# Two tiles of tokens per expert step, with the weights as the stationary operand

## The chip, the cores and the metric

The kernel runs on one core of one Trainium2 chip. The metric is the device time of one execution in microseconds (us); lower is better. Engines are named as in the profile: PE is the matrix engine (PEld its weight loads), DVE the vector engine, ACT the scalar engine, POOL the general engine, SP the queue engine that issues most DMAs.

## The reference

A batch of 32 images (3 x 96 x 96) is cut into 36 patches each, turned into 192-wide tokens, and joined with 128 text tokens: 32 x 164 = 5248 tokens. Then comes one attention block with a decaying state, and a mixture of experts, on which the change works:

```python
xn = _rms_norm(x, norm_w)
xf = xn.reshape(-1, D)                       # 5248 tokens x 192
logits = xf @ router_w.T                     # 8 experts
probs = jax.nn.softmax(logits, axis=-1)
_, top_idx = jax.lax.top_k(probs, TOP_K)     # 2 experts for each token
sel = jax.nn.one_hot(top_idx, N_EXPERTS, dtype=probs.dtype).sum(axis=1)
comb_w = probs * sel
g = jnp.einsum('td,efd->tef', xf, gate_w)    # 192 -> 384 in each expert
u = jnp.einsum('td,efd->tef', xf, up_w)
h = jax.nn.silu(g) * u
h = h * comb_w[:, :, None]
y = jnp.einsum('tef,edf->td', h, down_w)     # 384 -> 192
return y.reshape(B, S, D) + residual
```

## The kernel before

The first 40% of the time makes the tokens, the attention and the routing. While it does so it prepares the expert weights in SBUF: `wa` holds gate and up of all experts, `wd` down. Each weight is kept as a high part (rounded to the format `fp32r`) and a low part (what the rounding left), and the same is done to the tokens (`xh`, `xl`) and to the hidden rows (`hth`, `htl`), so that a few cheap products make up one exact one. POOL scatters each token, once for each of its two experts, to a table `disp` in DRAM, sorted by expert (L793).

Then come 89 **slots** (`SLOTS`): a slot is 128 rows of one expert. Experts have whole numbers of slots; which expert and which row of `disp` a slot has stands in `tab`, which DVE makes from the counts. A slot goes through this:

- SP loads its 128 rows into one of four buffers `xs` (L480, L482).
- PE turns the rows over with two transposes (L1084); ACT rounds them to `xh` (L738), DVE takes the rest `xl` (L1586).
- PE makes gate and up: `xh` and `xl` are the stationary operand, and 384 columns of weights stream past, in five products each for gate and for up (L1095 to L1099).
- ACT makes silu(gate) into `sg` (L741), DVE multiplies it by up into `hh` (L1590).
- `hh` has tokens on its partitions. The product with `down` needs hidden units there, so PE transposes it in three pieces (L1106); ACT rounds to `hth` (L744), DVE takes `htl` (L1593).
- PE makes the result in three pairs of products, 384 and 192 columns (L1115, L1117); ACT copies its low half (L750), DVE adds the halves (L1600).
- POOL copies the slot's row numbers (L820) and scatters the result to `ydram` (L823).

The order is written out by hand in `pipeline`: in step k PE does the rows of slot k+2, gate and up of k+1, the hidden transposes of k and the result of k-1, and each other engine the same in its own parts. A hardware loop runs four steps per turn. Waits are on counting semaphores.

After the last slot's rows are loaded, SP waits by `behind_slots` until enough results are stored and loads them back, sorted by token: first those of each token's lower expert (L400), then those of the upper one (L395). ACT scales them (L760), DVE adds them up, and SP and ACT store the output (L407). The thresholds of these waits stand in `ready`, which DVE computes from the counts.

```python
high, low, rest = (wa[:, bass.ds(e * (6 * DE) + 2 * DE * r + DE * which, DE)] for r in range(3))
pe.matmul(acc, xh[o][:, 0:P], high, start=True, stop=False)      # out[token, unit]: rows stationary
...
pe.transpose(bank[4][:, P * c:P * c + P], hh[b][:, P * c:P * c + P], ident[:])
```

Of the kernel before, what the change touches and what calls it, by code (L numbers as in the profile page):

```python
# [15 lines left out]
P = 128  # L16
B = 32
D = 192
# [22 lines left out]
TAB = SLOTS + 2  # L41
# [35 lines left out]
GUARDED = 8  # L77
# [38 lines left out]
def build(nc, pixels, bands, text, W, bias, attn_w, par, norm_w, router_w, gu_w, down_w, consts, out):  # L116
    with ExitStack() as ctx:
# [44 lines left out]
        wa5 = wa[:].rearrange("p (e r w f) -> p e r w f", e=NE, r=3, w=2)  # L162
# [23 lines left out]
        xh = [at(f"xh{i}", [P, 2 * P], F32R, r_ffn + 1024 * i) for i in range(2)]  # L186
        xl = [at(f"xl{i}", [P, 2 * P], F32R, r_ffn + 2048 + 1024 * i) for i in range(2)]
        sg = [at(f"sg{i}", [P, DE], F32, r_ffn + 4096 + 1536 * i) for i in range(2)]
        hh = [at(f"hh{i}", [P, DE], F32, r_ffn + 7168 + 1536 * i) for i in range(2)]
        hth = [at(f"hth{i}", [P, DE], F32R, r_ffn + 10240 + 1536 * i) for i in range(2)]  # L190
        htl = [at(f"htl{i}", [P, DE], F32R, r_ffn + 13312 + 1536 * i) for i in range(2)]
        ysb = [at(f"ysb{i}", [P, D], F32, (r_ffn + 16384 if i < 2 else r_gh + 6144 - 1536) + 768 * i) for i in range(DEPTH)]
        ylo = [at(f"ylo{i}", [P, D], F32, r_ffn + 17920 + 768 * i) for i in range(2)]
# [7 lines left out]
        slotf = sb("slotf", [P, 3, TAB])  # L201
        tabf = sb("tabf", [P, TAB, NE])
        ct = sb("ct", [P, 8, NE])
        cti = sb("cti", [P, 2, NE], I32)
        guard = sb("guard", [P, 2], I32)
# [61 lines left out]
        xs = [sb(f"xs{i}", [P, 2 * P + 3]) for i in range(2)]  # L267
        xs += [at(f"xs{i}", [P, 2 * P + 3], F32, r_ffn + 19456 + 1056 * (i - 2)) for i in range(2, DEPTH)]
        prow = xs[0][0:NPATCH, 0:D]
# [50 lines left out]
        s_xs = [sem(f"xs_in{i}") for i in range(DEPTH)]  # L320
# [25 lines left out]
        def pipeline(eng, step, parts, ahead, peel=0):  # L346


            first, last = -max(ahead), SLOTS - 1 - min(ahead)
            lo = -min(ahead) + (-min(ahead)) % 2 + peel  # L350
            n = (SLOTS - max(ahead) - lo) // DEPTH

            def there(k):
                return "".join(p for p, a in zip(parts, ahead) if 0 <= k + a < SLOTS)

            for k in range(first, lo):
                step(k, k % DEPTH, there(k))
            with eng.Fori(0, n) as i:
                for b in range(DEPTH):
                    step(DEPTH * i + (lo + b), (lo + b) % DEPTH)  # L360
# [1370 lines left out]
```

## Time and profile before

| | us |
|---|---|
| median of 3 runs | 540.99 (539.36 to 543.78) |
| the profiled execution, its own time | 540.32 |
| its span, first to last instruction | 538.6 |
| first gate product of the slots to last result product | 229.3 to about 511 |
| after the last PE product to the end | about 27 |
| PE busy in the whole span | 480.9 (89%) |

The slots take a little over half of the span. A row of the profile names a line, an engine, an operation and the tiles by name. Starts of PE instructions are measured; their ends are a model, so the distance between two starts says more than a duration does.

### The profile page before, as it was taken

Reading aid. Unit: us, or ns where it says so; the run is one execution under the profiler, and the core shown is the slowest. Engines: PE = TensorE matmul, PEld = TensorE weight load, DVE = VectorE, ACT = ScalarE, POOL = GpSimd, SP = SyncE. Lnnn points to the kernel's source line nnn. Section 1 sums busy time; section 2 is a strip of 40 time slices with the busy share of each in tenths; the row PEclk is TensorE's granted clock in tenths of the full one; section 3 lists DMA queues with packets and bytes.
Section 4 is the critical chain, followed back from the end, with each engine's and each line's share of the span. In section 5 each row is a group of like instructions: output and inputs, shape, how many; then the busy total and the mean of one; then the engine's idle time right before and its main releaser. Section 6 shows DMA issues by size and latency. Waiting matters only on the chain.

```text
span 538.6 us, 12568 instructions
## 1 busy us (share of the span) xinstructions
PE 480.9 (89%) x3157; PEld 456.8 (85%) x3158; DVE 375.9 (70%) x1295; ACT 304.9 (57%) x773; POOL 189.0 (35%) x272
## 2 busy tenths in 40 slices
PE   1999999999898985999999999999999999999800
PEld 1999998777777775899999999999999999999800
DVE  4969996658998899676665565566556556655596
ACT  5493977847788876345444544444454444445473
POOL 1000000004777776753333433333343333334320
PEclk9999999999999999799999999999999999999965
DMA  8989622311433431742222222222223222225897
GB/s 306 413 349 374 186 106 88 149 45 52 119 119 93 140 97 67 171 111 74 72 83 69 69 78 76 69 76 79 69 69 82 72 69 70 84 69 165 262 353 229
DMA packets 62463, 71.67 MB, mean 133 GB/s; under 512 B 19057, under 2 KB 56626, under 8 KB 61410
## 3 DMA queue, kind: packets, MB, share of 16 engines
q1 hardware_dynamic: 49920, 51.43, 31.5%
q0 software_dynamic: 8208, 16.95, 8.8%
q10 hardware_dynamic: 4306, 2.95, 2.0%
q8 instruction: 13, 0.21, 0.2%
q14 instruction: 16, 0.13, 0.1%
HBM read 49.43 MB, written 21.86 MB: 132 GB/s over the span
## 4 chain that ended last, share of the span: by engine, by line
PE 69%; DVE 17%; DMA 6%; ACT 3%; issue 2%; ACTq 1%; SPq 0%; POOL 0%; DVEq 0%; POOLq 0%
PE bank L849 8%; PE pair L849 6%; PE bank L1095 5%; PE bank L1099 5%; PE bank L1097 5%; PE bank L1096 5%; PE bank L1098 5%; PE bank L1106 5%; PE bank L1115 4%; PE pair L1115 4%; PE pair L1084 3%; ACT yall L760 2%; DMA ydram<-ysb,dnow 2%; DVE hres L1373 2%; PE bank L1117 2%
## 5 line engine op out<-in xcount | busy, mean ns | idle before, releaser
L793 POOL DMA_INDIRECT disp<-xf,posu x82 | 82.1, 1001 | 151.6 <-ACT xf L671 128.4
L1590 DVE TENSOR_TENSOR hh<-sg,bank 128x384 f32<-128x384 f32 x89 | 49.3, 554 | 99.3 <-ACT sg L741 99.3
L823 POOL DMA_INDIRECT ydram<-ysb,dnow x89 | 88.5, 994 | 69.5 <-DMA ydram<-ysb,dnow 36.6
L741 ACT ACTIVATE sg<-bank 128x384 f32<-128x384 f32 x89 | 43.8, 492 | 116.4 <-PE bank L1099 116.4
L1095 PE MATMUL bank<-wa,xh 128*128 x178 | 67.6, 380 | 0.0
L1099 PE MATMUL bank<-wa,xl 128*128 x178 | 60.1, 338 | 0.0
L1097 PE MATMUL bank<-wa,xl 128*128 x178 | 59.9, 336 | 0.0
L1096 PE MATMUL bank<-wa,xh 128*128 x178 | 59.8, 336 | 0.0
L1098 PE MATMUL bank<-wa,xh 128*128 x178 | 59.6, 335 | 0.0
L820 POOL COPY dnow<-dest 128x1 uint32 (+1 forms) x89 | 16.6, 187 | 107.4 <-DVE ysb L1600 97.7
L849 PE MATMUL bank<-wcT,imgT 128*128 128x193 f32 x240 | 42.5, 340 | 11.0 <-DMA imgT<-in_pixels 11.0
L849 PEld LDWEIGHTS bank<-wcT,imgT 128*128 128x128 f32 x240 | 41.9, 199 | 10.7 <-issue 10.7
L1593 DVE TENSOR_TENSOR htl<-bank,hth 128x384 fp32r<-128x384 f32 x89 | 48.9, 550 | 0.9 <-ACT hth L744 0.9
L1115 PE MATMUL pair<-wd,hth 128*128 x135 | 44.6, 379 | 0.4 <-DVE htl L1593 0.4
L1106 PE MATMUL bank<-ident,hh 128*128 128x128 f32 x267 | 43.6, 272 | 0.6 <-DVE htl L1593 0.6
L1115 PE MATMUL bank<-wd,hth 128*128 x132 | 44.1, 383 | 0.0
L744 ACT CAST hth<-bank 128x384 fp32r<-128x384 f32 x89 | 42.4, 476 | 0.8 <-PE bank L1106 0.8
L1106 PEld LDWEIGHTS bank<-ident,hh 128*128 128x128 f32 x267 | 34.5, 140 | 3.8 <-DVE hh L1590 0.8
L1586 DVE TENSOR_TENSOR xl<-pair,xh 128x256 fp32r<-128x256 f32 x89 | 37.2, 418 | 0.4 <-ACT xh L738 0.4
L994 PE MATMUL pair<-nst,xT 96*128 96x208 f32 x164 | 35.9, 340 | 1.7 <-DVE z L1382 1.0
L738 ACT CAST xh<-pair 128x256 fp32r<-128x256 f32 x89 | 33.5, 377 | 4.5 <-PE pair L1084 4.5
L1084 PE MATMUL pair<-ident,xs 128*128 128x128 f32 x178 | 34.0, 273 | 1.5 <-DVE xl L1586 1.3
(262 smaller groups left out, 1163.8 us busy)
## 6 DMA issues: line engine op xcount, KB each, us to landing
xs<-disp SPq DMA_DIRECT2D x89, 96.0 KB, 2.0
band<-in_bands SPq DMA_DIRECT2D x4, 1536.0 KB, 12.1
yall<-ydram SPq DMA_DIRECT2D x7, 768.0 KB, 7.6
imgT<-in_pixels SPq DMA_DIRECT2D x4, 768.0 KB, 12.9
imgT<-in_pixels SPq DMA_DIRECT2D x2, 1536.0 KB, 16.0
hres<-in_text SPq DMA_DIRECT2D x1, 3072.0 KB, 26.1
wa<-in_gate_up_w SPq DMA_DIRECT2D x8, 384.0 KB, 5.8
ring<-in_gate_up_w SPq DMA_DIRECT2D x32, 96.0 KB, 2.9
```

Source lines behind the costliest of these rows:

```text
L793: pool.indirect_dma_start(disp, bass.IndirectOffsetOnAxis(ap=posu[xbuf(c)][:, 2 * j + k:2 * j + k + 1], axis=0), xfd[xbuf(c)][:, j, :], No ...
L823: pool.indirect_dma_start(ydram, bass.IndirectOffsetOnAxis(ap=dnow[b][:], axis=0), ysb[r][:], None).then_inc(s_ys[b], 16)
L849: ins = pe.matmul(bank[PATCH_BANK[p % 4]][:, 0:193], imgT[:, 2 * i + dr, j + s, c, :], wcT[:, k, :], start=(k == 0), stop=(k == 23))
L1084: ins = pe.transpose(bank[5][:, P * m:P * m + P], xs[x][:, P * m:P * m + P], ident[:])
L1095: pe.matmul(acc, xh[o][:, 0:P], high, start=True, stop=False)
L1096: pe.matmul(acc, xh[o][:, 0:P], low, start=False, stop=False)
L1097: pe.matmul(acc, xl[o][:, 0:P], high, start=False, stop=False)
L1098: pe.matmul(acc, xh[o][:, P:2 * P], rest, start=False, stop=False)
L1099: ins = pe.matmul(acc, xl[o][:, P:2 * P], rest, start=False, stop=True)
L1106: ins = pe.transpose(bank[4][:, P * c:P * c + P], hh[b][:, P * c:P * c + P], ident[:])
L1115: pe.matmul(bank[6 + o][:, 0:2 * D], hth[o][:, P * c:P * c + P], wd[:, both], start=(c == 0), stop=False)
L1590: v.tensor_tensor(hh[o][:], sg[o][:], bank[2 * o + 1][:, 0:DE], ALU.mult).then_inc(s_hh, 1)
```

## The change

68 of the 89 slots are now run two at a time, as 34 **pair** steps of 256 rows; the other 21 stay single (**lone**): 6 at the front, 15 at the end. There are 55 steps in all (`ITEMS`). In a pair step:

- The weights are the stationary operand and 256 token columns stream past. The hidden units are cut into three blocks of 128 (index c); each has five products for gate and five for up, 30 in all. The output has hidden units on its partitions already, so the hidden transposes are gone; `hth` and `htl` are made from `hh` in SBUF.
- The stationary operand is not read from `wa` but from one buffer `wnow`, into which SP copies the step's expert from `wa` by DMA, SBUF to SBUF, in three pieces of 128 partitions x 3072 bytes. A piece is copied anew in each step, as soon as the same piece was last used in the step before.
- One buffer `xs` holds 256 rows, of two such buffers. SP loads the rows of step i+2 ahead of the copies of step i.
- Each of the two results still takes three pairs of products, as before.

The layout of `wa` goes by blocks now (`wa6`), so its preparation reads and writes three pieces where it had one, with DMA rows of 1024 and 512 bytes instead of 3072 and 1536. DVE makes the table for pairs and for the lone slots at the end with more, smaller instructions. The order of the work is another: all full pairs by expert, as far as 34 + 3 of them go, then the single tiles of the experts, then the rest of the last experts. The thresholds in `ready` follow from that.

The core of the diff:

```diff
+FULL = (TILES * 2 - NE) // 2
+FIRST = 6
+PAIR0, PAIR1 = FIRST, FIRST + FULL - FIRST // 2
+NLONE = SLOTS - 2 * FULL
+ITEMS = PAIR1 + NLONE
...
+        wnow = at("wnow", [P, FC * GU], F32R, r_gh + 9280)
...
+            def load_pair(s, b):
+                free_at = s - 2 if isinstance(s, int) and s == PAIR0 else s - 1
+                sp.wait_ge(s_xst, free_at)
+                sp.wait_ge(s_dest, free_at)
+                row = sp.value_load(tab[0:1, 0, bass.ds(s, 1)], min_val=0, max_val=NE * REGION)
+                rows = disp[bass.ds(row, W2), :].rearrange("(j p) d -> p j d", j=2)
+                sp.dma_start(xs[b][:, :, 0:D], rows[:, :, 0:D]).then_inc(s_xs[b], 16)
+                sp.dma_start(xs[b][:, :, D:2 * P + 3], rows[:, :, D1:DROW]).then_inc(s_xs[b], 16)
...
+            def copy_expert(i):
+                e = sp.value_load(tab[0:1, 1, bass.ds(i, 1)], min_val=0, max_val=NE - 1)
+                for c in range(FC):
+                    if late_enough(i, PAIR0 + 1):
+                        sp.wait_ge(s_gu, blocks(i) + (c - 2))
+                    sp.dma_start(wnow[:, GU * c:GU * c + GU].bitcast(F32),
+                                 wa[:, bass.ds(e * (FC * GU) + GU * c, GU)].bitcast(F32)).then_inc(s_wnow[c], 16)
...
+            def turn(i, b):
+                load_pair(i + 2, b)
+                copy_expert(i)
...
+            def gate_up_pair(i, b):
+                pe.wait_ge(s_xlo, i + 1)
+                x = [(xh[b][:, W2 * m:W2 * m + W2], xl[b][:, W2 * m:W2 * m + W2]) for m in range(2)]
+                for c in range(FC):
+                    at_front = isinstance(i, int) and i == PAIR0
+                    pe.wait_ge(s_hh, blocks(i) + (min(c - 1, 0) if at_front else c - 2))
+                    pe.wait_ge(s_wnow[c], 16 * i + (16 - 16 * PAIR0))
                     for which in range(2):
+                        high, low, rest = (wnow[:, GU * c + W2 * r + P * which:GU * c + W2 * r + P * which + P] for r in range(3))
+                        acc = bank[c][:, W2 * which:W2 * which + W2]
+                        pe.matmul(acc, high, x[0][0], start=True, stop=False)
+                        pe.matmul(acc, high, x[0][1], start=False, stop=False)
+                        pe.matmul(acc, low, x[0][0], start=False, stop=False)
+                        pe.matmul(acc, rest, x[1][0], start=False, stop=False)
+                        ins = pe.matmul(acc, rest, x[1][1], start=False, stop=True)
                     ins.then_inc(s_gu, 1)
...
             def step(i, b):                                  # DVE's
+                if is_pair(i):
+                    for c in range(FC):
+                        o = slice(W2 * c, W2 * c + W2)
+                        v.wait_ge(s_sg, blocks(i) + (c + 1))
+                        v.tensor_tensor(hh[b][:, o], sg[:, o], bank[c][:, W2:2 * W2], ALU.mult).then_inc(s_hh, 1)
+                        if c == FC - 1 and (is_pair(i + 2) or is_lone(i + 2)):
+                            rows_low(i + 2, b)
+                        v.wait_ge(s_hth, blocks(i) + (c + 1))
+                        v.tensor_tensor(htl[b][:, o], hh[b][:, o], hth[b][:, o].bitcast(F32), ALU.subtract
+                                        ).then_inc(s_htl, 1)
```

`blocks(i)` is how many signals of gate and up precede step i (one for a lone slot, three for a pair); so the wait in `copy_expert` is for piece c of step i-1. In step i PE does gate and up of i, the row transposes of i+2, and the two results of i-1.

On PE, in the loop, one slot of before had gate and up (its last three products are shown), the hidden transposes, the result, and the row transposes of a later slot:

```order
L1097 MATMUL bank<-wa,xl_87 128x384
L1098 ISA
L1098 MATMUL bank<-wa,xh_85 128x384
L1099 MATMUL bank<-wa,xl_87 128x384
L1102 REGISTER_ALU
L1104 REGISTER_ALU
L1106 MATMUL bank<-ident,hh_90 128x128 x3
L1115 ISA
L1115 MATMUL bank<-wd,hth_93 128x384
L1117 MATMUL bank<-wd,htl_95 128x192
```

Now a pair step has six groups of five products with 256 columns each (one is shown), then the row transposes, then the results; a product is named after its line, and `bank<-xh,wnow` has the weights stationary:

```order
L1211 MATMUL bank<-xh_84,wnow 128x256
L1212 MATMUL bank<-xl_86,wnow 128x256
L1213 MATMUL bank<-xh_84,wnow 128x256
L1214 MATMUL bank<-xh_84,wnow 128x256
L1215 MATMUL bank<-xl_86,wnow 128x256
...
L1188 MATMUL pair<-ident,xs_168 128x128 x4
L1239 ISA
L1242 ISA
L1247 ISA
L1247 MATMUL pair<-wd,hth_91 128x384
L1248 MATMUL pair<-wd,htl_89 128x192
```

The three hidden transposes of a slot left the loop; 20 products of 384 columns for two slots became 30 of 256; the results stayed as they were.

On SP, in its loop, a slot of before had two loads and one read of the table:

```order
L479 TENSOR_LOAD tab
L479 ISA x2
L480 ISA
L480 DMA xs_168<-disp 128x192
L482 ISA
L482 DMA xs_168<-disp 128x67
```

A pair step has two loads of twice the size, and the copies behind them:

```order
L513 TENSOR_LOAD tab
L515 DMA xs_169<-disp 128x2x192
L517 ISA
L517 DMA xs_169<-disp 128x2x67
L538 ISA
L538 TENSOR_LOAD tab
...
L542 DMA wnow<-wa 128x768
L541 REGISTER_ALU
L542 ISA
L542 DMA wnow<-wa 128x768
```

The copies share SP's queue with the row loads, and stand behind those of two steps later.

## Rows read from the trace of the kernel before

**Rows 1.** The page: busy time of PE, and its busy tenths in 40 slices.

```profile
PE 480.9 (89%) x3157; PEld 456.8 (85%) x3158; DVE 375.9 (70%) x1295; ACT 304.9 (57%) x773; POOL 189.0 (35%) x272
...
PE   1999999999898985999999999999999999999800
```

**Rows 2.** The page: the chain that ended last, by engine.

```profile
PE 69%; DVE 17%; DMA 6%; ACT 3%; issue 2%; ACTq 1%; SPq 0%; POOL 0%; DVEq 0%; POOLq 0%
```

**Rows 3.** Windows, amid the slots: us, five engines busy, PEclk, DMA share, GB/s.

```profile
340.00:360.00 20.00, 20.00 (x136) 19.79 (x135) 11.67 (x31) 9.71 (x26) 7.95 (x13) 1.00 0.26 72
```

**Rows 4.** Timeline of one slot, PE and PEld: start us, us, instruction.

```profile
350.71 0.43 PE L1095 MATMUL bank<-wa,xh 128*128 x1
...
351.67 0.33 PE L1095 MATMUL bank<-wa,xh 128*128 x1
...
352.54 0.49 PE L1106 MATMUL bank<-ident,hh 128*128 128x128 f32 x3
...
353.05 0.25 PE L1117 MATMUL bank<-wd,htl 128*128 x1
...
353.34 0.25 PE L1117 MATMUL bank<-wd,htl 128*128 x1
353.34 0.19 PEld L1115 LDWEIGHTS bank<-wd,hth 128*128 128x128 f32 x1
...
353.45 0.19 PEld L1117 LDWEIGHTS bank<-wd,htl 128*128 128x128 f32 x1
353.63 0.25 PE L1117 MATMUL bank<-wd,htl 128*128 x1
...
353.72 0.38 PE L1084 MATMUL pair<-ident,xs 128*128 128x128 f32 x2
...
353.86 0.42 PE L1095 MATMUL bank<-wa,xh 128*128 x1
```

**Rows 5.** The page: costliest groups on DVE, ACT and POOL, with mean ns of one.

```profile
L1590 DVE TENSOR_TENSOR hh<-sg,bank 128x384 f32<-128x384 f32 x89 | 49.3, 554 | 99.3 <-ACT sg L741 99.3
L823 POOL DMA_INDIRECT ydram<-ysb,dnow x89 | 88.5, 994 | 69.5 <-DMA ydram<-ysb,dnow 36.6
L741 ACT ACTIVATE sg<-bank 128x384 f32<-128x384 f32 x89 | 43.8, 492 | 116.4 <-PE bank L1099 116.4
...
L1586 DVE TENSOR_TENSOR xl<-pair,xh 128x256 fp32r<-128x256 f32 x89 | 37.2, 418 | 0.4 <-ACT xh L738 0.4
...
L738 ACT CAST xh<-pair 128x256 fp32r<-128x256 f32 x89 | 33.5, 377 | 4.5 <-PE pair L1084 4.5
```

**Rows 6.** The page: DMA issues, KB each, us to landing.

```profile
xs<-disp SPq DMA_DIRECT2D x89, 96.0 KB, 2.0
...
wa<-in_gate_up_w SPq DMA_DIRECT2D x8, 384.0 KB, 5.8
...
ydram<-ysb,dnow POOLq DMA_INDIRECT x89, 2.6
```

**Rows 7.** DMA rate, 88 to 102 us in 40 slices, only the eight `wa` loads run.

```profile
GB/s 0 0 0 0 0 0 0 184 176 132 272 281 360 395 413 386 386 386 360 360 342 386 413 395 421 413 325 395 418 404 404 351 184 53 18 0 0 0 0 0
```

**Rows 8.** Timeline of the first slots, DVE: start us, us, instruction, idle before it.

```profile
228.12 0.22 DVE L1581 SCALAR_TENSOR_TENSOR dest<-xs,slotf 128x1 uint32<-128x1 f32 x1 [4.14 <-PE pair L1084]
...
234.82 0.61 DVE L1504 TENSOR_TENSOR tabf<-cst,ct 128x440 f32<-128x440 f32 x1
...
237.77 0.60 DVE L1510 TENSOR_TENSOR tabf<-tabf,ct 128x440 f32<-128x440 f32 x1
```

**Rows 9.** Timeline of the first slots, ACT.

```profile
235.65 0.49 ACT L741 ACTIVATE sg<-bank 128x384 f32<-128x384 f32 x1 [0.72 <-PE bank L1099]
...
239.08 0.49 ACT L741 ACTIVATE sg<-bank 128x384 f32<-128x384 f32 x1 [1.24 <-PE bank L1099]
```

**Rows 10.** The chain that ended last, where the slots end.

```profile
501.63 6.51 DMA ydram<-ysb,dnow
...
508.20 4.69 DMA yall<-ydram
```

More of the change, by code:

```diff
@@ L344, in wcol, with items, is_pair, is_lone @@
             return WPIECE[dr + 1]
[L346 to L360, printed above, removed]
-            for k in range(lo + DEPTH * n, last + 1):
-                step(k, k % DEPTH, there(k))
+        def items(eng, step):
+            lo = PAIR0 + 2
+            n = (PAIR1 - 2 - lo) // 2
+            for i in range(-2, lo):
+                step(i, i % 2)
+            with eng.Fori(0, n) as k:
+                for b in range(2):
+                    step(2 * k + (lo + b), (lo + b) % 2)
+            for i in range(lo + 2 * n, ITEMS + 2):
+                step(i, i % 2)
+        def is_pair(i):
+            return not isinstance(i, int) or PAIR0 <= i < PAIR1
+        def is_lone(i):
+            return isinstance(i, int) and (0 <= i < PAIR0 or PAIR1 <= i < ITEMS)
+        def late_enough(i, least):
+            return not isinstance(i, int) or i >= least
+        def blocks(i):
+            if is_pair(i):
+                return 3 * i - 2 * PAIR0
+            return i if i < PAIR0 else 3 * PAIR1 - 2 * PAIR0 + (i - PAIR1)
+        def tile_of(i):
+            if is_pair(i):
+                return 2 * i - PAIR0
+            return i if i < PAIR0 else 2 * PAIR1 - PAIR0 + (i - PAIR1)
+        def quarter(i):
+            return (i + 2) % 4 if i < PAIR0 else (i - PAIR1) % 4
+        def lone_xs(i):
+            return xs[quarter(i) // 2][:, quarter(i) % 2, :]
+        def lone_loads(i):
+            return len([k for k in range(i + 1) if is_lone(k) and quarter(k) == quarter(i)])
+        def lone_banks(i):
+            return (bank[0], bank[1]) if i % 2 == 0 else (bank[2], bank[4])
         def of_group(row, g):
@@ L488, in _ @@
                     sp.wait_ge(s_tab, 2)
-                if s >= DEPTH:
-                    done.append([sp.value_load(ready[0:1, s - DEPTH, b:b + 1], min_val=16, max_val=16 * ((SLOTS + 1) // 2))
-                                 for b in range(2)])
+                    for f in range(4):
+                        done.append([sp.value_load(ready[0:1, f, b:b + 1], min_val=16, max_val=16 * ((SLOTS + 1) // 2))
+                                     for b in range(2)])
             def behind_slots(f):
@@ new lines, in down @@
+            def down(reg, b, g, p, first, step_c, ready_at):
+                e = pe.snap(reg, min_val=0, max_val=NE - 1)
+                pe.wait_ge(s_htl, ready_at)
+                if late_enough(g, 2):
+                    pe.wait_ge(s_y, g - 1)
+                for c in range(FC):
+                    o = first + step_c * c
+                    both = bass.ds(e * (FC * 2 * D) + c * 2 * D, 2 * D)
+                    high = bass.ds(e * (FC * 2 * D) + c * 2 * D, D)
+                    pe.matmul(bank[6 + p][:, 0:2 * D], hth[b][:, o:o + P], wd[:, both], start=(c == 0), stop=False)
+                    ins = pe.matmul(bank[6 + p][:, 0:D], htl[b][:, o:o + P], wd[:, high], start=False, stop=(c == FC - 1))
+                ins.then_inc(s_dn, 1)
@@ L1127, in _ @@
+            items(pe, step)
         @block.vector
@@ L1490, in _ @@
             v.wait_ge(s_cread, 1)
-            cnt, til, cum, gap, one = (ct[:, k, :] for k in range(5))
+            cnt, til, cum, gap, one, full2, odd, cumo = (ct[:, k, :] for k in range(8))
             st.mark(v.memset(one, 1.0))
@@ L1607, in _ @@
+            items(v, step)
             v.wait_ge(s_upd, TILES)
```

426 lines of the change are left out of this document (269 added, 157 removed).

## The prediction

> **What bounds the kernel now.** I read the page first. PE is busy for 89% of the span, and in the slices from 230 us on it is full [rows 1]; the chain that ended last lies 69% on PE [rows 2]. Amid the slots the window shows PE busy for 20.00 of 20 us at a granted clock of 1.00, which is its 2.4 GHz level, DVE for 11.67, ACT for 9.71, POOL for 7.95, and the DMA engines for 0.26 of their time [rows 3]. So in the slots only PE's own stream counts, and the change is worth what it takes from that stream, as long as nothing else becomes late. The timeline of one slot gives the prices, by distances between starts [rows 4]:
>
> - a slot takes 353.86 - 350.71 = 3.15 us, two take 6.30;
> - a product with 384 columns takes (352.54 - 351.67) / 5 = 0.174 us;
> - a result pair (384 and 192 columns) takes 0.29 us, so its product with 192 columns 0.116;
> - from the first hidden transpose to the first row transpose are 353.72 - 352.54 = 1.18 us; less three result pairs (0.87) leaves 0.31, or 0.10 for a hidden transpose;
> - the two weight loads at 353.34 and 353.45 start 0.11 apart, the closest that loads follow each other here.
>
> **Products and transposes, per pair.** Removed: 20 products x 0.174 = 3.48 us and 6 hidden transposes x 0.10 = 0.62. The four row transposes and six result pairs stay. Added: 30 products with 256 columns, for which there is no row. At 2.4 GHz 384 columns stream in 0.160, so 0.014 comes on top; 256 columns stream in 0.107, and with the same 0.014 they take 0.121, a little over the 0.11 of a weight load, which then just hides. The bounds: no product can follow faster than weights are loaded, 0.11; the straight line from 192 columns (0.116, where the load and not the stream may have set the pace) to 384 (0.174) gives 0.135. I take 0.121, since 192 columns stream in 0.080 and their 0.116 can be explained by the load alone. Then 30 x 0.121 = 3.63, and a pair step takes 6.30 - 3.48 - 0.62 + 3.63 = 5.83 us, 0.47 less than two slots. Over 34 steps: 16 us. With 0.11 it is 27 us, with 0.135 it is 2 us. That both kernels stream the same columns for gate and up (7680 for two slots) shows where the gain can come from: from the transposes, and not from the products, which cost 0.15 us more.
>
> The Trainium skill, "TensorE: Matmul & The Clock Gate", section "Back-to-back issue gap", gives columns / 2.4 + 2.5 ns for the distance of products; by that 256 columns take 109 ns, and the gain would be 28 us. The rows above show 174 ns for 384 columns where the formula has 162.5, so I don't follow it; it stands near my lower bound.
>
> **The copies.** A piece c of `wnow` may be overwritten when PE is through with it in step i-1, and is needed one step later, less its own block of ten products: 5.83 - 1.21 = 4.6 us. A piece is 393 KB. A row load of 96 KB lands in 2.0 us [rows 6]; 295 KB more at some 386 GB/s, the plateau of the loads of 3072-byte rows with all engines at work [rows 7], add 0.8. So 2.8 us, well under 4.6. In sum the DMA engines now work 0.26 x 6.30 = 1.6 us per two slots [rows 3, 4]; 1.18 MB of copies add 3.1; 4.7 us of a step of 5.83 is 80%. The releases come 1.2 us apart and a piece keeps the engines for 1.0, so they do not pile up. SP issues five transfers per step where it issued four, with one more table read, and has the row loads of step i+2 ahead of them; those wait only for transposes done two steps earlier, so nothing stands in the way of the copies. That is estimated at no cost. What no row shows is a transfer from SBUF to SBUF; all rows are from DRAM. If the copies came late, PE would stand at the piece's first product, with the results of the step before behind it.
>
> **ACT, DVE, POOL.** A pair has on DVE the same elements as two slots (hh and htl 1536, the row parts 512, the results 384) in the same ten instructions; on ACT nine instead of eight. So their 11.67 and 9.71 of 20 us [rows 3] become some 63% and 53% of the shorter step. The one chain with a deadline is from the last block of step i-1 to its result, which PE comes to after all 30 products and four row transposes of step i, 4.0 us later. One after another: silu under 0.49, hh under 0.55, the row parts (twice the width of 0.377 and 0.418) 0.75 and 0.84, hth under 0.49, htl under 0.55, in sum 3.7 at most [rows 5]; some of it runs in parallel. It is hidden, with the smallest margin of all. POOL's two scatters at 0.99 us each fit.
>
> **The front.** DVE makes more small instructions for `ready`, but it has 4.14 us of idle time before the first slot's rows [rows 8], so these are free. The table of the far slots is made between slots: 2 and 6 instructions, the large ones 0.6 us each [rows 8]; the slot around them took 239.08 - 235.65 = 3.43 us, 0.28 more than the steady 3.15 [rows 9]. Now there are about 22 small ones in two places. At about 0.2 each they are 4.4 us where there were 3.1; I take 1 us of loss, bounds 0 and 2. The preparation of `wa` moves the same bytes in shorter rows, and its loads are issued early: 0, at most 1 us.
>
> **The end.** The upper results are loaded when the stores up to a threshold have landed; now the last of these takes 6.51 us to land and the load behind it 4.69 [rows 10]. By the counts that the reference's inputs give, this threshold was 84 stored slots and becomes 85, because three odd tiles of other experts stand before the rest of the last expert. One slot is 3.15 us at most, but the next store is already under way: I take 1.5, bounds 0 and 3.
>
> **The sum** for the profiled execution: 540.3 - 16 + 1 + 1.5 = 526.8. The median of before is 0.7 above its profiled execution, so 527.5, and I give 527. The bounds of the product give 516 and 541.
>
> **Rivals.**
>
> 1. Products with 256 columns take 0.135 or more, so that what the transposes gave is eaten up. For it speaks the straight line through two measured lengths; against it that the shorter of them can be limited by its weight load. 34 x 0.05 = 2 us gained, 2.5 lost: 541, no change. The same result comes if the chain over ACT and DVE is late by 0.4 us in each step. Chance together 0.17.
> 2. Slower: the copies land too late. The place is the wait for `wnow` ahead of a block, and it decides from a landing time of 4.6 us; from 5.1 the kernel is slower than before. For it: the same 384 KB took 5.8 us in the eight loads of `wa` [rows 6], and a store took 6.51 instead of 2.6 while large loads ran [rows 6, 10]; SBUF would be read and written at once. Against it: those loads were queued behind each other, and the copies are not. With 5.8 us a step takes 5.8 + 1.2 = 7.0, 0.7 more than two slots: 24 us, plus 2.5, or 567. Chance 0.12.
> 3. Weight loads don't hide. Then a product takes 0.107 + 0.11 = 0.217, 30 take 6.5, and the kernel loses 2.4 us per step: 624. The measured 0.174 for 384 columns has room for 0.160 of streaming and nearly nothing else, and every product has its own load. Chance 0.02. The Trainium skill, same page, section "The mechanism", says that a weight load overlaps running products only when the row groups differ; by that rule this rival would be the case, and the trace disagrees with it at 0.174 us.
> 4. The change doesn't do what it says: excluded, since the loop has 34 fixed pair steps, and the order of instructions shows no hidden transposes in them.
>
> **How the numbers follow.** My forecast has a chance of 0.69 and its own range from 516 to 535 (products of 0.11 to 0.128). A difference under 1%, 5.4 us, is about what a measurement of this kernel can't tell from no change. Faster by more: 0.69 and a little of rival 1, 0.72. Within 1%: 0.14. Slower: 0.14, from rivals 2 and 3 with their milder forms. The range of 514 to 546 takes in rival 1 and leaves out 0.14.
>
> **What the profile after would show.** Right: first products of two pair steps 5.8 us apart, products 0.12 apart, `wnow` copies landing in about 3 us, PE idle nowhere in the loop, DMA share about 0.8. Wrong: products 0.13 or more apart (rival 1); idle time of PE or its weight loads released by a DMA of `wnow` (rival 2); idle time released by DVE's htl (the chain over ACT and DVE); slots at the front more than 1 us longer than before; the first upper load more than 3 us later against the last product.

## The result, and the profile after

The changed kernel takes 526.28 us, the median of 4 runs (526.12 to 526.65), against 541.01 for the kernel before (4 runs, 539.36 to 543.78). The ratio is 0.9724, 95% interval 0.9683 to 0.9764: 14.7 us faster. Five more executions, beside the experiments, gave 526.06 and 0.9722 (0.9680 to 0.9763). A sixth of these took 534.47 us at a granted clock of 0.955, where the others have 0.963 to 0.972, and isn't counted. The profiled execution took 526.12 us with a span of 524.4; before it was 540.32 and 538.6.

The page of the kernel after, busy time of the engines, the 40 slices of PE and of the DMA engines, and the chain by engine, answers to [rows 1, 2]:

```profile
PE 462.1 (88%) x3293; PEld 438.4 (84%) x3294; DVE 376.8 (72%) x1314; ACT 314.6 (60%) x807; POOL 189.0 (36%) x272
...
PE   1999999999899897799999999999999998999800
...
DMA  8998630611433342455777888888888877226897
...
PE 63%; DVE 18%; DMA 7%; ACT 4%; issue 3%; SPq 2%; ACTq 1%; DVEq 0%; POOL 0%; POOLq 0%
```

PE is still full where the slots run, and is busy for 18.8 us less in all; the share of the DMA engines has risen to 0.7 to 0.8 in the slices of the pair steps. The 2% of SPq in the chain are new: they lie between 244 and 280 and between 420 and 450 us, where transfers were issued late. The window that answers to [rows 3] (us, the five engines busy, PEclk, DMA share, GB/s):

```profile
340.00:360.00 20.00, 20.00 (x163) 20.00 (x163) 13.43 (x37) 11.98 (x34) 8.15 (x14) 1.00 0.85 296
```

DVE and ACT, at 67% and 60%, have become busier, and PE waits for neither. Against [rows 4], the timeline of PE and of its weight loads in a pair step:

```profile
350.01 0.28 PE L1211 MATMUL bank<-xh,wnow 128*128 128x256 f32 x1
350.13 0.28 PE L1212 MATMUL bank<-xl,wnow 128*128 128x256 f32 x1
350.24 0.28 PE L1213 MATMUL bank<-xh,wnow 128*128 128x256 f32 x1
...
350.60 0.28 PE L1211 MATMUL bank<-xh,wnow 128*128 128x256 f32 x1
```
```profile
350.01 0.19 PEld L1212 LDWEIGHTS bank<-xl,wnow 128*128 128x128 f32 x1
350.13 0.19 PEld L1213 LDWEIGHTS bank<-xh,wnow 128*128 128x128 f32 x1
```

Five products take 350.60 - 350.01 = 0.59 us, 0.118 each, and the weight load of the next starts with each of them. How long a step takes is seen at the first silu of each (timeline of ACT):

```profile
344.53 0.38 ACT L828 ACTIVATE sg<-bank 128x256 f32<-128x256 f32 x1 [0.88 <-PE bank L1215]
...
350.21 0.38 ACT L828 ACTIVATE sg<-bank 128x256 f32<-128x256 f32 x1 [0.88 <-PE bank L1215]
```

It is 5.68 us. The groups of the page that answer to [rows 5], and the DMA issues, to [rows 6]:

```profile
L1799 DVE TENSOR_TENSOR hh<-sg,bank 128x256 f32<-128x256 f32 x102 | 42.4, 416 | 33.9 <-ACT sg L828 33.8
...
L1211 PE MATMUL bank<-xh,wnow 128*128 128x256 f32 x204 | 58.5, 287 | 3.6 <-DMA wnow<-wa 3.6
L828 ACT ACTIVATE sg<-bank 128x256 f32<-128x256 f32 x102 | 38.8, 380 | 34.1 <-PE bank L1215 33.9
...
wnow<-wa SPq DMA_DIRECT2D x102, 384.0 KB, 2.7
```

A copy lands in 2.7 us (median). In all of the loop PE waits for copies 3.6 us, four times, and all four lie in the first four pair steps or the last three.

**Where the time went.** The starts of the silus cut the span in the same places in every kernel. The table has the differences in us; "first four" and "last four" are pair steps, or the eight slots in their place.

| stretch | before | after | difference |
|---|---|---|---|
| start to first silu | 231.40 | 230.94 | -0.5 |
| six lone slots at the front | 17.62 | 19.72 | +2.1 |
| first four pair steps | 25.15 | 25.52 | +0.4 |
| 26 pair steps in between | 163.45 | 147.87 | -15.6 |
| last four pair steps | 25.15 | 24.80 | -0.3 |
| last 14 lone slots | 43.82 | 43.46 | -0.4 |
| last silu to the end | 31.97 | 32.06 | +0.1 |

So the 26 steps in between take 5.69 us each for 6.29 before. Had all eight steps at the two ends done the same, each four would take 22.7 us: 2.8 us are lost in the first four and 2.1 in the last four, beside 2.1 in the lone slots ahead of them.

### The profile page after: what moved, and what is told of

The parts are those of the page before. It is cut to its first block, busy times and chain, and to the rows that moved or that the text cites. A ratio compares the mean times of both kernels' runs of the same rounds, so it can differ in the third digit from the quotient of the medians.

```text
span 524.4 us, 12468 instructions
## 1 busy us (share of the span) xinstructions
PE 462.1 (88%) x3293; PEld 438.4 (84%) x3294; DVE 376.8 (72%) x1314; ACT 314.6 (60%) x807; POOL 189.0 (36%) x272
## 4 chain that ended last, share of the span: by engine, by line
PE 63%; DVE 18%; DMA 7%; ACT 4%; issue 3%; SPq 2%; ACTq 1%; DVEq 0%; POOL 0%; POOLq 0%
PE bank L950 8%; PE pair L950 6%; PE bank L1211 4%; PE bank L1215 4%; PE bank L1213 4%; PE bank L1212 4%; PE bank L1214 4%; PE bank L1247 4%; PE pair L1247 4%; PE pair L1188 3%; ACT yall L861 3%; DMA wnow<-wa 2%; PE bank L1029 2%; DVE hres L1525 2%; DVE stats L1539 2%
## 5 line engine op out<-in xcount | busy, mean ns | idle before, releaser
L1799 DVE TENSOR_TENSOR hh<-sg,bank 128x256 f32<-128x256 f32 x102 | 42.4, 416 | 33.9 <-ACT sg L828 33.8
L1803 DVE TENSOR_TENSOR htl<-hh,hth 128x256 fp32r<-128x256 f32 x102 | 43.0, 422 | 32.1 <-ACT hth L835 32.1
L835 ACT CAST hth<-hh 128x256 fp32r<-128x256 f32 x102 | 41.4, 406 | 35.7 <-DVE hh L1799 35.6
L1211 PE MATMUL bank<-xh,wnow 128*128 128x256 f32 x204 | 58.5, 287 | 3.6 <-DMA wnow<-wa 3.6
L828 ACT ACTIVATE sg<-bank 128x256 f32<-128x256 f32 x102 | 38.8, 380 | 34.1 <-PE bank L1215 33.9
L1215 PE MATMUL bank<-xl,wnow 128*128 128x256 f32 x204 | 57.3, 281 | 0.0
L1213 PE MATMUL bank<-xh,wnow 128*128 128x256 f32 x204 | 57.2, 281 | 0.0
L1212 PE MATMUL bank<-xl,wnow 128*128 128x256 f32 x204 | 57.2, 281 | 0.0
L1214 PE MATMUL bank<-xh,wnow 128*128 128x256 f32 x204 | 57.2, 281 | 0.0
L1247 PE MATMUL pair<-wd,hth 128*128 x135 | 44.5, 379 | 0.4 <-DVE htl L1782 0.4
L1211 PEld LDWEIGHTS bank<-xh,wnow 128*128 128x128 f32 x204 | 38.5, 189 | 4.8 <-issue 2.0
L1247 PE MATMUL bank<-wd,hth 128*128 x132 | 41.5, 364 | 0.0
L1212 PEld LDWEIGHTS bank<-xl,wnow 128*128 128x128 f32 x204 | 38.7, 189 | 0.0
L1214 PEld LDWEIGHTS bank<-xh,wnow 128*128 128x128 f32 x204 | 38.6, 189 | 0.0
L1215 PEld LDWEIGHTS bank<-xl,wnow 128*128 128x128 f32 x204 | 38.5, 189 | 0.0
L1213 PEld LDWEIGHTS bank<-xh,wnow 128*128 128x128 f32 x204 | 38.5, 189 | 0.0
```

Source lines behind the costliest of these rows:

```text
L835: nc.scalar.copy(hth[b][:, W2 * c:W2 * c + W2], hh[b][:, W2 * c:W2 * c + W2]).then_inc(s_hth, 1)
L1211: pe.matmul(acc, high, x[0][0], start=True, stop=False)
L1212: pe.matmul(acc, high, x[0][1], start=False, stop=False)
L1213: pe.matmul(acc, low, x[0][0], start=False, stop=False)
L1214: pe.matmul(acc, rest, x[1][0], start=False, stop=False)
L1215: ins = pe.matmul(acc, rest, x[1][1], start=False, stop=True)
```

## The experiments

They ran in three groups; the kernel before, beside them, took 540.76, 540.65 and 542.04 us. Single executions of one kernel differ by up to 7.5 us (the changed kernel: 522.59 to 530.06), and in the profiles of the table the first silu starts anywhere from 228.9 to 233.7 us, before the edited code is reached. So beside each time I read the same stretches as above. Each stands for one profiled execution. A second trace of the changed kernel (e8) has 19.62, 24.62, 5.69 and 24.70 us in the four columns, so a difference of under 1 us in the first four steps can be chance.

| kernel | median us (runs) | six lone | first four | 26 steps, each | last four |
|---|---|---|---|---|---|
| after | 526.28 (4) | 19.72 | 25.52 | 5.69 | 24.80 |
| e1 copies first | 525.66 (6) | 18.14 | 24.95 | 5.77 | 23.27 |
| e2 one copy | 520.93 (4) | 19.75 | 22.76 | 5.68 | 22.74 |
| e3 transposes back | 543.42 (10) | 20.20 | 26.14 | 6.22 | 26.06 |
| e4 widths | 523.5 (1) | 19.48 | 24.27 | 5.64 | 24.98 |
| e5 late table | 526.31 (6) | 19.67 | 28.70 | 5.68 | 24.68 |
| e6 order at ends | 527.09 (5) | 18.27 | 26.79 | 5.68 | 26.48 |
| e7 both | 526.83 (5) | 20.09 | 26.40 | 5.69 | 23.88 |
| e9 turn early | 527.3 (5) | 18.68 | 25.88 | 5.72 | 25.13 |
| e10 rows first | 525.76 (5) | 17.61 | 26.31 | 5.69 | 24.78 |
| e11 extra 384 KB | 547.07 (4) | 18.07 | 27.26 | 6.30 | 27.97 |
| e12 extra 1152 KB | 593.5 (1) | 18.31 | 33.07 | 7.83 | 29.60 |

**e3: what the gain is made of.** The six transposes per step that the change removed are put back, everything else stays.

```
+                    pe.wait_ge(s_htl, blocks(i - 1) + 3)
+                    for c in range(2 * FC):
+                        pe.transpose(bank[3][:, P * (c % FC):P * (c % FC) + P], hh[1 - b][:, P * c:P * c + P], ident[:])
```

> Puts six transposes of hidden rows, 128x128, back into 33 of the 34 pair steps, ahead of the two results; nothing reads their output. Theory A (the gain is the hidden transposes that left PE's stream, 0.109 us each): 33 x 6 x 0.109 = 21.6 us, so 548, slower than the kernel before by 7 us. Rival B (the gain is that of the products with the weights stationary, and transposes are cheap beside them): under 10 us, at most 536.

543.42 us, ratio to before 1.0046 (1.0023 to 1.0069): the whole gain is gone. The added transposes have a line of their own in the timeline of PE:

```profile
358.73 0.28 PE L1212 MATMUL bank<-xl,wnow 128*128 128x256 f32 x1
...
359.07 0.28 PE L1215 MATMUL bank<-xl,wnow 128*128 128x256 f32 x1
359.19 0.60 PE L1188 MATMUL pair<-ident,xs 128*128 128x128 f32 x4
359.62 0.82 PE L1266 MATMUL bank<-ident,hh 128*128 128x128 f32 x6
360.20 0.42 PE L1247 MATMUL pair<-wd,hth 128*128 x1
```

They take 0.109 us each, 0.65 a step, and 34 steps make 22 us. The kernel lost only 17.1, because its products are 0.113 apart (358.73 to 359.07 is three of them) where the changed kernel has 0.118; 30 x 0.0045 is 0.14 us a step, 4.6 in all. So the removal of the transposes is what the change gains, as the prediction had it, and the products themselves cost a little (30 x 0.118 = 3.54 us where 20 x 0.174 were 3.48). Why they follow closer here is taken up below.

**e2: what the copies cost.** Only the first step's copies are made; all later steps use that expert's weights (the copies of the last two pair steps, behind the loop, are left out too).

```
             def turn(i, b):
                 load_pair(i + 2, b)
-                copy_expert(i)
...
-                    pe.wait_ge(s_wnow[c], 16 * i + (16 - 16 * PAIR0))
+                    pe.wait_ge(s_wnow[c], 16)
```

> Leaves out the copies of all pair steps but the first, so all pair steps use one expert's gate and up weights; the stream of PE is the same. Theory A (the copies cost only the four late ones): 522.7, products still 0.118 us apart, steps 5.68 us apart. Rival B (40 MB of copies slow down PE's reads of SBUF or the other transfers): products closer to 0.109 us, 34 x 30 x 0.009 = 9 us more, about 514.

520.93 us (519.23 to 522.7). The steady step is 5.68 us as before, and both ends are at 22.7 to 22.8: the copies cost 2.8 + 2.1, or 4.8 us unrounded, at the ends and nothing in between (3.8 by the second trace of the changed kernel). The windows of the two kernels, after and then e2:

```profile
300.00:350.00 50.00, 50.00 (x406) 50.00 (x406) 32.87 (x89) 28.73 (x80) 20.25 (x36) 1.00 0.84 290
```
```profile
300.00:350.00 50.00, 50.00 (x407) 50.00 (x406) 32.95 (x89) 28.93 (x81) 20.84 (x35) 1.00 0.29 82
```

At a DMA share of 0.84 or of 0.29, PE issues the same number of instructions. The products don't follow closer either, which refutes that the traffic sets their 0.118. What e2 doesn't bring back are the 2.1 us of the lone slots (19.75), so the later copies don't cause them; the first step's copies, which stand behind the rows of that step, are still made here.

**e11 and e12: the margin of the copies.** In each of SP's turns in the loop stands one further transfer, of 384 KB or 1152 KB.

```
             def turn(i, b):
                 load_pair(i + 2, b)
                 copy_expert(i)
+                sp.dma_start(scrap[bass.ds(i * P, P), :], wa[:, 0:1 * GU].bitcast(F32)).then_inc(s_scrap, 16)
```

> The changed kernel, with one further transfer of 384 KB (a piece of wa to a scratch in DRAM) behind the three copies in each of SP's 30 turns in the loop. DMA work per step goes from 4.7 us of 5.68 (0.83) to about 5.7: at the edge. Theory A (the copies have a margin of 0.8 us a step): products wait for wnow in nearly every step, by 0 to 0.6 us, 530 to 545 us. Theory B (the busy share says little, the queues overlap): no change, 526.3 within 1 us.

> The same with 1152 KB a turn, so that DMA work per step is 4.7 + 3.1 = 7.8 us against 5.68. Theory A (the DMA engines' rate is the limit once the share passes 1): a step takes 7.8 us, 30 of them 64 us more, 590 us, and PE waits for wnow in each. Theory B (not limited by the rate): under 545.

(e12 takes the columns `0:3 * GU` instead.) 547.07 us (545.91 to 547.39) and 593.5, the latter in one execution. The waits are those of theory A; its time is met in e12 (590), and passed by 2 us in e11 (530 to 545). A step takes 6.30 and 7.83 us. First the window of e11 and PE's waits there between 300 and 400 us (us in total, times, longest), then the same of e12:

```profile
300.00:350.00 50.00, 46.44 (x365) 44.43 (x364) 29.06 (x80) 25.43 (x72) 18.99 (x32) 1.00 0.90 321
```
```profile
PE bank L1215 <- DMA wnow<-wa: 7.3, 16, 0.6
```
```profile
300.00:350.00 50.00, 42.01 (x307) 40.38 (x305) 25.23 (x68) 22.39 (x62) 14.22 (x24) 0.93 0.99 353
```
```profile
PE bank L1215 <- DMA wnow<-wa: 18.7, 13, 2.2
```

(L1215 here is the product that is L1211 in the changed kernel.) In e12 the engines are full, and 353 GB/s x 7.83 us is 2.8 MB: the 1.65 MB of the changed kernel's step (290 GB/s x 5.68) and the 1.18 added. The clock was at its lower level in part of that stretch (0.93), but PE waits for copies for 18.7 of 100 us, so the clock didn't set the pace. In e11 the share reaches only 0.90, and yet PE waits once in every step (16 times in 100 us). That is rival 2 of the prediction, produced on purpose: one more piece per step, and the kernel is slower than before (ratio 1.0088, 1.0062 to 1.0114). The copies of the change are free in the steady loop, with less than one piece of room. Whether the room is that of the DMA engines or that of SP's queue, where each such transfer takes 0.49 us to issue, e11 doesn't separate.

**e1, e6 and e9: why the copies are late at the ends.** The changed kernel's SP queue where the loop begins (timeline of SP):

```profile
250.50 0.38 SPq L515 DMA_DIRECT2D xs<-disp  x1
251.08 0.37 SPq L517 DMA_DIRECT2D xs<-disp  x1
252.69 2.00 SPq L542 DMA_DIRECT2D wnow<-wa  x3
```

and the two waits of PE that follow in the first four steps:

```profile
256.36 0.35 PE L1211 MATMUL bank<-xh,wnow 128*128 128x256 f32 x1 [1.00 <-DMA wnow<-wa]
...
268.98 0.39 PE L1211 MATMUL bank<-xh,wnow 128*128 128x256 f32 x1 [1.16 <-DMA wnow<-wa]
```

The first silu of the step before starts at 250.66, so piece 0 was free by then; its copy was issued at 252.69, behind both row loads and their table reads. I took SP's order for the cause. e1 puts the copies ahead of the loads everywhere, in the loop and for the last two pair steps:

```
             def turn(i, b):
-                load_pair(i + 2, b)
                 copy_expert(i)
+                load_pair(i + 2, b)
```

> SP issues the copies of step i ahead of the row loads of step i+2 (in the loop, and for the last two pair steps ahead of the lone loads); nothing else changes. Theory A (the four waits of PE for wnow, 3.6 us together, come from SP's order: a copy stands in the queue behind a row load that waits or is slow): the waits go, 526.3 becomes about 522.7, and no wait for xs takes their place, since rows then have one step and a half to land. Rival B (the copies are late because they land late under DMA traffic): the four waits stay, 526 within 0.5 us. Rival C (the rows are now late): waits for xs appear at the row transposes, slower than 526.3.

525.66 us (524.92 to 530.43), ratio 0.9752 (0.9709 to 0.9794): no change. The ends won 0.6 and 1.5 us and the loop lost 0.08 x 26 = 2.0. What e1 has instead of waits for copies, in the waits of PEld and PE over the whole span:

```profile
PEld bank L1211 <- issue: 5.3, 14, 0.9
...
PEld pair L1188 <- DMA xs<-disp: 3.3, 3, 1.7
...
PE bank L1211 <- DMA wnow<-wa: 1.0, 2, 0.7
```

"issue" stands for PE's own sequencer. At the end of a step it reads the expert two steps on from the table (L1275), which takes 0.89 us (median of 18) in e1, 0.72 in the changed kernel and 0.30 in e2. The read ends 0.6 to 1.0 us before the first weight load of the next step in e1, 1.3 to 1.6 in the changed kernel; that the sequencer is late for this reason fits these numbers, but no run shows it. e6 changes the order at the two ends alone, where alone there was something to win:

```
+            for i in range(PAIR0 + 1, PAIR0 + 3):
+                copy_expert(i)
+                load_pair(i + 2, i % 2)
...
+                if i in (PAIR1, PAIR1 + 2):
+                    copy_expert(PAIR1 - 2 + (i - PAIR1) // 2)
                 load_lone(i)
-                if i in (PAIR1 + 1, PAIR1 + 3):
-                    copy_expert(PAIR1 - 2 + (i - PAIR1) // 2)
```

> The changed kernel, with SP's order changed at the two ends alone: the copies of pair steps 1 and 2 (items 7 and 8) stand ahead of the rows of items 9 and 10, and the copies of the last two pair steps (items 38 and 39) ahead of the lone rows 40 and 42; the loop in between is as it was. Theory A (the four late copies, 3.6 us together, come from the place in SP's queue at the two ends, where the first e1 run's loss in the loop isn't): the waits of PE at L1211 for wnow fall from 3.6 to under 1.5 us and the time falls by about 2 us, to 524.3. Theory B (the DMA engines are simply full there, 0.83 of them busy, and order only moves the wait from copies to rows): waits for xs appear in their place, and the time stays within 0.7 us of 526.3.

527.09 us (524.49 to 529.07), and the ends are longer than before the edit, 26.79 and 26.48 us. At the front the wait moved to where the order changes back: the loads of items 10 and 11 now stand one behind the other ahead of the copies of item 9 (loads at 260.92 and 262.94, copies from 264.95), and PE waits 2.9 us for them. At the end PE waits 1.9 us for one copy, and the granted clock is 0.53 between 442 and 445 us. e7 below has the same order there, waits 0.7 us at a clock of 1.00 and takes 23.88 us, so the 26.48 aren't shown to come from the order. e9 moves the gate of the row loads, the transposes, one block earlier, so that loads and then copies could start earlier:

```
+                    if c == FC - 2 and (is_pair(i + 2) or is_lone(i + 2)):
+                        turn_rows(i + 2, b)
...
-                    if is_pair(i + 2) or is_lone(i + 2):
-                        turn_rows(i + 2, b)
```

> The changed kernel, with the four transposes of the rows two steps ahead between the second and the third block of products instead of behind the third. The same work on TensorE. Theory A (the row loads are gated by these transposes, so they and the copies behind them in SP's queue start 1.2 us earlier in every step, and the four late copies at the ends go): waits for wnow under 1.5 us in all, 2 us less, 524.3. Theory B (the copies are gated by the block before last, not by the transposes, so nothing moves; the rows must only be there 1.2 us earlier): 526.3 within 1 us. Beside it the products' spacing: if the steps lock at 118 ns since nothing breaks up their row of 30, some are 113 or 114 ns here, and each step that is gains 0.14 us.

527.3 us (526.36 to 529.62); PE's waits for `wnow` are 3.8 us as before. Theory B holds. So the order in SP's queue decides which transfer is late, but no order tried here makes none late. That the copies cost the time at the ends is shown (e2 has no loss there). Between 250 and 272 us a copy lands in 3.2 us (median of 11) where the loop has 2.7, and SP issues it 2.0 us after its piece is free where the loop has 0.8; which of the two comes first, and from what, stays open.

**e5, e7 and e10: the lone slots at the front.** e5 takes the table of the later slots off the lone slots 0 and 1:

```
-                if isinstance(i, int) and 0 <= i <= 5:
-                    between(i)
+                if isinstance(i, int) and 2 <= i <= 7:
+                    between(i if i <= 5 else i - 6)
```

> The changed kernel, with the guard and table operations on VectorE (some 20 short ones, 0.6 us each) taken from between the lone steps 0 to 5 of the start and put behind steps 2 to 7, so that steps 0 and 1 carry none. Theory A (the lone steps at the start lost 2.1 us because VectorE, which now also has the rows of a step further ahead, carries these between the slots): the gaps between the silus of the lone steps fall back from 3.7 to 3.8 towards 3.2 us, and the time falls by 1 to 2 us, to about 524.6. Theory B (they are late for transfers and start-up, not for the table): no change within 0.5 us, 526.3. Theory C: the later table holds TensorE's first table read at step 6 and it is slower by over 1 us.

526.31 us (523.54 to 529.53), ratio 0.9732 (0.9700 to 0.9765). The silus show both halves of the story (ACT; in the changed kernel they start at 232.92, 235.57, 239.28, 243.00 and 246.84):

```profile
231.95 0.49 ACT L842 ACTIVATE sg<-bank 128x384 f32<-128x384 f32 x1 [0.78 <-PE bank L1234]
234.48 0.49 ACT L842 ACTIVATE sg<-bank 128x384 f32<-128x384 f32 x1 [0.96 <-PE bank L1234]
237.66 0.49 ACT L842 ACTIVATE sg<-bank 128x384 f32<-128x384 f32 x1 [0.96 <-PE bank L1234]
240.78 0.49 ACT L842 ACTIVATE sg<-bank 128x384 f32<-128x384 f32 x1 [0.92 <-PE bank L1234]
245.29 0.49 ACT L842 ACTIVATE sg<-bank 128x384 f32<-128x384 f32 x1 [1.53 <-PE bank L1234]
```

Without the table a slot takes 3.12 to 3.18 us where it took 3.71, and then two take 4.51 and 4.35: all of it is given back before the first pair step. The rows of the first pairs don't come earlier, and PE waits for them (`xs`) and for the first copies. The first four pair steps take 28.70 us, 3.2 more. PE waits 3.5 us for copies there, where the changed kernel waited 2.2. Then comes something that the edit didn't aim at, seen in the windows of e5 and, last, of the changed kernel:

```profile
268.00:271.00 3.00, 1.31 (x11) 1.31 (x12) 1.94 (x7) 1.15 (x4) 0.41 (x2) 1.00 0.53 182
271.00:274.00 3.00, 3.00 (x16) 3.00 (x16) 1.16 (x3) 1.17 (x3) 1.97 (x3) 0.50 0.74 247
```
```profile
271.00:274.00 3.00, 3.00 (x27) 3.00 (x26) 2.02 (x7) 2.15 (x6) 0.98 (x1) 1.00 0.73 278
```

PE had been busy for 1.31 of 3 us, the granted clock fell to its 1.2 GHz level, and PE issued 16 instructions where it issues 27. The fourth pair step took 7.19 us instead of 5.74, so by my estimate 1.4 of the 3.2 us are the clock's. The moved table instructions themselves (0.14 to 0.28 us each) hold up DVE once, for 0.4 us. e7 joins e5 and e6.

> Both edits of the two runs before together. If both theories A hold: 4 us less than the changed kernel, about 522.3; if neither does, 526.3 within 1 us. The sum of the two runs alone is what independent causes would give.

526.83 us (526.12 to 527.99): the two edits add nothing to each other. e10 keeps the late table and loads the rows of both first pairs ahead of the first copies:

```
             load_pair(PAIR0, 0)
-            copy_expert(PAIR0)
             load_pair(PAIR0 + 1, 1)
+            copy_expert(PAIR0)
```

> The kernel with the late table, and SP's first two row loads of pairs (items 6 and 7) both ahead of the copies of item 6. Theory A (with the table gone the lone steps run at 3.12 us, and what took the 2.1 us back were rows of item 7 that stood behind three copies in SP's queue): the waits of PEld and PE for xs between 240 and 260 us fall from 3 to under 1 us, and 2 us less than the late table alone, 524.3. Theory B (the DMA engines carry all they can at that place, 0.87 busy from 240 to 246 us): the wait turns up at wnow of item 6 instead, 526.3 within 1 us.

525.76 us (524.29 to 527.4), ratio 0.9696 (0.9668 to 0.9724). Now the six lone slots take 17.61 us, what they took before the change, and between 236 and 262 us PE waits 0.2 us for rows and PEld 0.4. That is theory A's half; the wait has turned up at a copy, as theory B had it: the first four pair steps are 0.8 us longer, with one wait of 1.9 us at L1211. The trace fits two causes that hide each other, the table and rows that stand behind three copies. Their sizes are not shown, for the same front differs from trace to trace: in e11 and e12, where neither is edited, the lone slots take 18.07 and 18.31 us and PE waits for no row in them, and in e3 and e4 they take 20.20 and 19.48 with waits of 1.2 and 1.0 us. It is the best whole kernel of the study by its ratio, but the interval overlaps that of the changed kernel, so I don't call it faster.

**e4: is it the columns that set the products' pace?** In the loop the three blocks of a step have products of 256, 224 and 192 columns; the columns that are missing aren't computed.

```
-                        acc = bank[c][:, W2 * which:W2 * which + W2]
+                        w = 256 if isinstance(i, int) else (256, 224, 192)[c]
+                        acc = bank[c][:, W2 * which:W2 * which + w]
+                        x = [(xh[b][:, W2 * m:W2 * m + w], xl[b][:, W2 * m:W2 * m + w]) for m in range(2)]
```

> In the 30 pair steps of the hardware loop the ten products of block 1 have 224 columns and those of block 2 have 192 instead of 256 (the rest of the rows of tokens is left out there). It measures what sets the distance of products. Theory A (streaming plus 0.011 us, with a floor at the 0.109 us of a weight load): block 0 at 0.118, blocks 1 and 2 both at 0.109 to 0.111, a step 0.16 us shorter, about 521.5. Rival B (streaming alone counts): 0.104 and 0.091, a step 0.41 shorter, about 514. Rival C (the weight load sets 0.118 already for 256 columns): all three at 0.118, 526.

523.5 us in one run; 146.65 us for the 26 steps, 0.05 less per step. The timeline of PE:

```profile
358.08 0.28 PE L1215 MATMUL bank<-xh,wnow 128*128 128x256 f32 x1
...
358.88 0.28 PE L1217 MATMUL bank<-xl,wnow 128*128 128x256 f32 x1
...
360.19 0.28 PE L1214 MATMUL bank<-xl,wnow 128*128 128x192 f32 x1
...
360.98 0.28 PE L1216 MATMUL bank<-xh,wnow 128*128 128x192 f32 x1
```

Seven products of 256 columns take 0.80 us, and seven of 192 take 0.79: 0.114 and 0.113. At 2.4 GHz 64 columns are 0.027, so if the stream set the pace, the second number would be 0.087. Here columns don't set the pace: there is a floor that each product with its weight load has. Over the 30 steps the products of 224 and 192 columns are 0.111 to 0.113 apart, those of 256 are 0.113 to 0.116 apart in 21 steps and 0.118 in nine. So the floor is 0.11, and 0.118 occurs at 256 columns alone. That the floor is the weight load's own time fits that loads start at the same distance; no run loads weights without a product, so it isn't shown. The Trainium skill's formula ("TensorE: Matmul & The Clock Gate", "Back-to-back issue gap") would give 82.5 ns for 192 columns, an estimate. The section itself says that the formula leaves out the weight load and gives too little for short products, and the trace agrees: 0.113 is more.

**e8: the changed kernel again.**

> The changed kernel unedited, on the same chip and between the same runs as the three others, so that they can be compared within one call: 526.3 us as before, within 1 us, and a ratio of 0.972 to the kernel before.

526.06 us (522.59 to 530.06). Its trace starts its first silu at 240.0 us, later than all others, and serves only to show how far the stretches of one kernel differ (above).

## Why the prediction was right, point by point

The forecast was 527, the time is 526.3, and the mechanism is the one forecast. That the number is met within 1 us is luck: behind the sum stand errors that cancel, 4.4 us too little gain in the steps against 4.8 us of late copies that were put at nothing.

1. **The step: right, and too careful.** Forecast 5.83 us with products of 0.121; measured 5.68 with 0.118. 30 x 0.003 is 0.09; the other 0.06 lie in the parts that I had as differences of starts. Over 34 steps the gain is 34 x (6.29 - 5.69) = 20.4 us, not 16: the term is mis-sized by 4.4 us. The reason I gave was half right. I put the pace at the stream (0.107 + 0.014) with the load "just hidden". e4 has products of 192 and of 256 columns at the same 0.113, so my reading of the result products with 192 columns (0.116, a pace that the columns don't set) could have been carried to 256 columns. That 256 columns take 0.118 in the changed kernel's loop and 0.113 in e3 neither reading explains.
2. **The copies: right in the loop, wrong at the ends.** Landing in 2.8 us was forecast, 2.7 is measured; the DMA share was forecast at 0.8, and it is 0.83 to 0.85. The step that failed is "nothing stands in the way of the copies. That is estimated at no cost": it is 4.8 us (e2), lost in the first four and the last four pair steps. I reckoned with a steady state alone. In the loop the first copy of a step is issued 3.5 us before PE needs it (356.71 against 360.17) and lands in 2.7, a margin of 0.8 us, not the 4.6 - 2.8 = 1.8 that I had from the moment the piece is free: SP came to the copy 0.8 us after its piece was free (first silu at 355.89), with the loads and their table reads ahead of it. With a margin that small, about 1 us decides whether a step waits. (SP has no more table reads than before, either: the prediction's "one more table read" sets the two of a pair step against the one of a single slot.)
3. **The front: 1 us forecast, 2.1 measured**, a little outside of my bounds. Without waits for rows it was 0.5 and 0.7 (e11, e12), inside them; the second reason beside the table, which I had not in the sum, is rows that stand behind three copies (e5, e10).
4. **The end: 1.5 us forecast, 0.1 measured, and that is partly luck.** The chain there, against [rows 10]:

```profile
482.88 6.43 DMA ydram<-ysb,dnow
...
490.48 3.42 DMA ydram<-ysb,dnow
...
493.92 4.78 DMA yall<-ydram
```

   As forecast, the last store that is waited for stands later: it starts 1.8 us before the last silu (492.3), where it was 5.0 (501.63 against 506.6). But it landed in 3.42 us instead of 6.51, so the load behind it starts 1.6 us after the last silu in both. In the other kernels, whose end is the same, the stretch behind the last silu takes 31.98 to 33.08 us. Why this store landed faster isn't shown.
5. **ACT, DVE, POOL: right.** 63% and 53% were forecast, 66% and 57% measured between 300 and 350 us, and PE waits for `htl` 0.4 us in the whole run (page, L1247). The chain with the smallest margin held.

The sum by the measured terms, which are stretches of the same two traces: 540.3 - 20.4 (34 steps) + 4.8 (copies at the ends) + 2.1 (front) + 0.1 (end) - 0.5 (start) - 0.4 (last slots) = 526.0, against 526.12.

The rivals: products at 0.135 (rival 1) didn't happen. Late copies (rival 2) happened in some of the eight steps at the two ends, and e11 shows how near it was for all: 384 KB more per step. Unhidden loads (rival 3) are refuted, with the rule of the Trainium skill ("TensorE: Matmul & The Clock Gate", "The mechanism") that would have made them so: each product has a load of its own, and both go at 0.118 us.

## What to carry to other kernels

When a PE stream is full, count instructions with their weight loads before columns: from 192 to 256 columns a product costs nearly the same here (0.112 to 0.118 us), so the way to win is to fill each load with 256 columns and to have fewer instructions, such as transposes that another operand order makes unnecessary. A transfer that is hidden in the steady loop must be checked for the first and the last steps apart, from when its queue comes to it and not from when its buffer is free. When an edit takes a stall away, read the same stretches in both traces before judging by the total: three of these edits removed the wait they aimed at, and each of the three gave it back a few us later. Read the granted clock of the stretch too: a wait of PE can cost a second time through it (e5).

## What the hardware showed that I had not expected

- The products of one pair step are all about 0.113 us apart, or all about 0.118, rarely mixed. In the changed kernel, in e2 and e10 nearly every step of the full loop is at 0.118; in e3, with six more transposes per step, every one is at 0.113 or 0.114; in e11, with a short wait in each step, most are at 0.113. The steps right behind a wait in the first four are often at 0.113 too. It is not DMA traffic (e2). Columns have a part in it: in e4 the narrower products never show 0.118, and those of 256 do in nine of 30 steps. In e9, where the row transposes break up the 30 products, most are still at 0.118. It is worth 0.14 us a step, 4.6 us a kernel, and what decides it stays open.
- A copy of 384 KB from SBUF to SBUF lands in 2.6 to 4.2 us, median 2.7, half of the 5.8 of the same size from DRAM when eight are queued [rows 6].
- A read of the table by a sequencer takes 0.27 us on SP's quiet moments (239.93) and 0.89 (244.32) behind three copies; on PE between 300 and 400 us it takes 0.56 to 0.75, 0.79 to 0.92 in e1, and 0.30 to 0.31 in e2, whose loop has no copies. It stands in no busy time.
